# Query and key pieces stored once per batch, with the bias table loaded in eight portions between the stores

## The reference, cut to what matters

```
xn = layernorm(x)
Q, K, V = (proj(Wq, bq), proj(Wk, bk), proj(Wv, bv))      # (16, 16 heads, 256, 8)
scores = einsum('bhqd,bhkd->bhqk', Q, K) / sqrt(8) + rel_bias[:, clip(q - k, -128, 128) + 128]
out = softmax(scores) @ V
x = x + (out @ Wo.T + bo) * silu(ffn0(xn))
```

## Time and profile before

| | us |
|---|---|
| median of 3 timed runs | 816.46 (813.6 to 817.75) |
| the profiled execution, its own time | 811.98 |
| its span, first to last instruction | 809.9 |
| PE, DVE, ACT, POOL busy | 696.4, 555.7, 487.4, 454.5 |

### The profile page before, as it was taken

The page is one execution under the profiler, slowest core; times in us unless marked ns, Lnnn a source line. Parts: engine busy times, 40 slices in busy tenths (PEclk is TensorE's granted clock), DMA queues, the critical chain, the costliest instruction groups (busy, mean ns, idle before and its releaser), DMA issues. The chain is left out here.

```text
span 809.9 us, 16884 instructions
## 1 busy us (share of the span) xinstructions
PE 696.4 (86%) x5338; PEld 477.2 (59%) x5338; DVE 555.7 (69%) x1292; ACT 487.4 (60%) x919; POOL 454.5 (56%) x398
## 2 busy tenths in 40 slices
PE   2876888899998999979999889899897688999970
PEld 1652222233332333338999878789887677998870
DVE  7787999999997999843343377835737894643454
ACT  1662677788886888866455537578661264554550
POOL 8930454599998999983544544410005776554451
PEclk9898899999999999989999999999998799999995
DMA  7997551132332232136887796560001424777936
GB/s 234 362 275 220 171 172 54 54 95 79 90 97 72 80 91 76 57 125 193 247 261 246 240 308 195 175 176 1 2 1 37 156 75 113 238 220 232 290 122 194
DMA packets 115377, 124.09 MB, mean 153 GB/s; under 512 B 10608, under 2 KB 97312, under 8 KB 115328
## 3 DMA queue, kind: packets, MB, share of 16 engines
q1 hardware_dynamic: 107200, 106.71, 44.0%
q0 software_dynamic: 8128, 16.78, 5.9%
HBM read 82.50 MB, written 40.81 MB: 152 GB/s over the span
## 5 line engine op out<-in xcount | busy, mean ns | idle before, releaser
L696 POOL DMA_INDIRECT yg_dram<-work x138 | 137.3, 995 | 145.5 <-DVE work L1817 123.2
L1276 ACT ACTIVATE work<-wide,work 128x256 f32<-128x256 f32 x324 | 131.7, 474 | 112.4 <-PE wide L914 111.3
L1427 DVE TENSOR_REDUCE work<-wide 128x4 bf16<-128x1024 f32 x128 | 155.9, 1226 | 22.7 <-PE wide L791 21.7
L925 PE MATMUL wide<-work 128*128 128x128 f32 x1296 | 157.6, 275 | 0.0
L925 PEld LDWEIGHTS wide<-work 128*128 128x128 f32 x1296 | 151.6, 192 | 0.8 <-ACT work L1276 0.3
L914 PE MATMUL wide<-xT,work 128*128 128x256 f32 x552 | 132.0, 382 | 9.6 <-issue 7.1
L914 PEld LDWEIGHTS wide<-xT,work 128*128 128x128 f32 x552 | 99.5, 190 | 23.4 <-issue 10.7
L659 POOL TENSOR_TENSOR work<-work,biasT 128x1024 f32<-128x1024 f32 x32 | 75.9, 2371 | 53.5 <-ACT work L1214 53.1
L659 POOL TENSOR_TENSOR yy<-yy,biasT 128x1024 f32<-128x1024 f32 x32 | 75.8, 2368 | 21.6 <-ACT yy L1214 21.0
L1221 ACT ACTIVATE yy<-yy 128x1024 f32<-128x1024 f32 x64 | 67.5, 1055 | 29.9 <-DVE yy L1695 26.2
L785 PE MATMUL wide<-biasA,turnb 128*128 128x512 bf16 x256 | 80.4, 397 | 5.7 <-DVE work L1427 5.3
(11 more groups left out here) (288 smaller groups left out, 1202.0 us busy)
## 6 DMA issues: line engine op xcount, KB each, us to landing
work<-in_wcat SPq DMA_DIRECT2D x73, 578.0 KB, 4.0
work<-stk_dram SPq DMA_DIRECT2D x128, 96.0 KB, 2.7
xg_dram<-empty SPq DMA_DIRECT2D x35, 260.0 KB, 2.8
work<-xg_dram SPq DMA_DIRECT2D x69, 130.0 KB
stk_dram<-yy SPq DMA_DIRECT2D x16, 384.0 KB, 3.4
stk_dram<-yy SPq DMA_DIRECT2D x16, 256.0 KB, 3.2
yy<-yg_dram SPq DMA_DIRECT2D x8, 512.0 KB, 6.5
biasT<-ext_dram SPq DMA_DIRECT2D x1, 3072.0 KB
```

The source lines that it names most:

```text
L696: g.indirect_dma_start(out=yg_dram[l], out_offset=bass.IndirectOffsetOnAxis(ap=yid[v][:, s_:s_ + 1].bitcast(u32), axis=0), in_=yb[u][:, s_ ...
L925: last = mm(YP[u][:, s_ * D:(s_ + 1) * D], hb[u][:, c, s_ * P:(s_ + 1) * P], wb[v][:, HID + c * D:HID + (c + 1) * D], start=(c == 0), stop ...
L1276: A(hb[u][:, c, :], bank[2 + 2 * u + c // 2][:, (c % 2) * TS:(c % 2 + 1) * TS], ACT.Gelu, bias=wb[v][:, bc:bc + 1]).then_inc(m["gelu"], 1)
L1427: V.tensor_reduce(nmax[:, :, 2 * place(t):2 * place(t) + 2].rearrange("p c e -> p e c"), into[:, :].rearrange("p (e c k) -> p e c k", e=2, ...
```

## The change

1. The six pieces of a batch are stored once, by one transfer (six rows of 512 bytes for each of 128 partitions), instead of twelve pieces by three transfers.
2. The columns of the query and key projections are put into another order (feature first, then head), by one ACT copy of the weights into `wqk_dh` and a seventh small weight transfer that brings the two bias columns in that order. PE's first projection waits for the copy.
3. The stacks are put together by the loads, which read a piece as often as it is needed: for each parity of heads three transfers (24, 16 and 8 partitions), each for queries and keys at once, in runs of 2 KB. That is six transfers instead of four for each half of a batch's heads; the bytes are the same.
4. `biasT` is loaded in eight portions of two heads, one behind each of the stores of batches 0 to 7, instead of by one transfer ahead of all stores.
5. The loads for batches 0 and 1 go out in halves, one behind each store of batches 8 to 15, instead of whole ones behind the stores of batches 8 to 11.

```
-STORES = len(RUNS)
+LOADS = 2 * len(RUNS)
...
-    stk_dram = nc.dram_tensor("stk_dram", [2, NB * D, TERMS, S], bf16, kind="Internal").ap()
+    stk_dram = nc.dram_tensor("stk_dram", [NB, 2 * NPIECE, D, S], bf16, kind="Internal").ap()
...
+            sp.dma_start(more[:, 2:4], wpack[:, WPACK - 5:WPACK - 3].rearrange("(h d) i -> d h i", d=DK)).then_inc(s_w, 16)
...
-            sp.dma_start(biasT[:, :, :], bass.AP(tensor=ext_dram.tensor, offset=0, ap=[[1, P], [EXT, H0], [1, BW]])
-                         ).then_inc(s_bt, 16)
+
+            def load_biasT(q):
+                sp.dma_start(biasT[:, q * 2:q * 2 + 2, :],
+                             bass.AP(tensor=ext_dram.tensor, offset=q * 2 * EXT, ap=[[1, P], [EXT, 2], [1, BW]])).then_inc(s_bt, 16)
...
-                a, r = list(pieces[u].ap), 0
-                for n in RUNS:
-                    dst = stk_dram[:, b * D:(b + 1) * D, r:r + n, :].rearrange("i d r s -> d i (r s)")
-                    src = bass.AP(tensor=pieces[u].tensor, offset=pieces[u].offset, ap=[a[0], [(6 - n) * S, 2], [1, n * S]])
-                    sp.dma_start(dst, src).then_inc(pre[0][f"stored{u}"], 16)
-                    r += n
-
-            def load_stacks(b, u, g):
-                for e in range(2):
-                    rows = slice(e * HALF, e * HALF + TROWS)
-                    ts = slice(g * 4, g * 4 + 4)
-
-                    def src(i):
-                        heads = stk_dram[i, b * D:b * D + D] if isinstance(b, int) else stk_dram[i, bass.ds(b * D, D)]
-                        return heads.rearrange("(a e t d) r s -> a e (d r) t s", a=2, e=2, d=DK)[g, e]
-                    sp.dma_start(qst[u][rows, ts, :], src(0)).then_inc(A0[f"stk{u}{g}"], 16)
-                    sp.dma_start(kst[u][rows, ts, :], src(1)).then_inc(A0[f"stk{u}{g}"], 16)
+                sp.dma_start(stk_dram[b].rearrange("r p s -> p r s"), pieces[u]).then_inc(pre[0][f"stored{u}"], 16)
+
+            def load_stacks(b, u, g, halves=(0, 1)):
+                for e in halves:
+                    heads = stk_dram[b if isinstance(b, int) else bass.ds(b, 1)]
+                    row = e * HALF
+                    for n in RUNS:
+                        dst = qst[u][row:row + n * DK, g * 4:g * 4 + 4, :]
+                        sp.dma_start(
+                            bass.AP(tensor=dst.tensor, offset=dst.offset, ap=[list(dst.ap)[0], [H0 // 2 * S, 2], [1, 4 * S]]),
+                            bass.AP(tensor=heads.tensor, offset=heads.offset + (g * 2 + e) * 4 * S,
+                                    ap=[[H0 * S, n * DK], [(2 * NPIECE - n) * D * S, 2], [1, 4 * S]])
+                        ).then_inc(A0[f"stk{u}{g}"], 16)
+                        row += n * DK
...
             for b in range(NB // 2):
                 store_pieces(b, b % NRING)
+                load_biasT(b)
...
                 first = b - NB // 2
-                if first < 2:
-                    sp.wait_ge(pre[0][f"stored{first}"], len(range(first, NB // 2, NRING)) * STORES * 16)
-                if first < 4:
-                    load_stacks(first // 2, first // 2, first % 2)
+                if first % 4 == 0:
+                    sp.wait_ge(pre[0][f"stored{first // 4}"], len(range(first // 4, b, NRING)) * 16)
+                load_stacks(first // 4, first // 4, first // 2 % 2, (first % 2,))
...
+                        pe.wait_ge(s_wo, 1)
...
-                        last = mm(bank[6 + u][:, i * S:(i + 1) * S], wqk_sb[:, i * D:(i + 1) * D], xT[u][:, :],
+                        last = mm(bank[6 + u][:, i * S:(i + 1) * S], wqk_dh[:, i * D:(i + 1) * D], xT[u][:, :],
...
             act.wait_ge(s_w, 16 * NW)
+            A(wqk_dh[:, :].rearrange("p (i d h) -> p i d h", i=2, d=DK),
+              wqk_sb.rearrange("p (i h d) -> p i d h", i=2, d=DK), ACT.Copy).then_inc(s_wo, 1)
```

More of the change, by code:

```diff
@@ L67 @@
 RUNS = (3, 2, 1)
+NPIECE = max(RUNS)
 TERMS = sum(RUNS)
@@ L197, in build @@
         shb_bc = sb("shb_bc", [P, D])
-        more = sb("more", [P, 2])
+        more = sb("more", [P, 4])
+        wqk_dh = sb("wqk_dh", [P, 2 * D])
         ext_sb, extr_sb, extb_sb = (yyf[0:H0, TOK + 6 * S + i * EXT:TOK + 6 * S + (i + 1) * EXT] for i in range(3))
@@ L305, in build @@
         bank = [wide[i // 2][:, i % 2 * 512:(i % 2 + 1) * 512] for i in range(8)]
-        bq_c, bk_c, bv_c, nw_c, temp_c = (cols[:, i:i + 1] for i in range(5))
-        bqs_c, et_c = (more[:, i:i + 1] for i in range(2))
+        bv_c, nw_c, temp_c = (cols[:, i:i + 1] for i in range(2, 5))
+        bqs_c, et_c, bq_c, bk_c = (more[:, i:i + 1] for i in range(4))
         s_x = [sem(f"x{q}_loaded") for q in range(4)]
-        s_w, s_wf = sem("weights_loaded"), sem("weights_folded")
+        s_w, s_wf, s_wo = sem("weights_loaded"), sem("weights_folded"), sem("projections_ordered")
         s_c = sem("constants_made")
@@ L359, in build @@
         A1 = phase_sems("attend", 1, ["x2", "C", "Cs", "U", "pr", "nn", "nns", "G", "gk", "GT", "gm", "mx", "exp", "rs", "an", "M", "Ms", "Pm", "Ps", "F", "s"])
-        NW = 6
+        NW = 7
         NEMPTY = EMPTIES
@@ L434, in _ @@
                 first = b - NB // 2
-                if first < 2:
-                    sp.wait_ge(pre[0][f"stored{first}"], len(range(first, NB // 2, NRING)) * STORES * 16)
-                if first < 4:
-                    load_stacks(first // 2, first // 2, first % 2)
+                if first % 4 == 0:
+                    sp.wait_ge(pre[0][f"stored{first // 4}"], len(range(first // 4, b, NRING)) * 16)
+                load_stacks(first // 4, first // 4, first // 2 % 2, (first % 2,))
             for u in range(NRING):
-                sp.wait_ge(pre[0][f"stored{u}"], len(range(u, NB, NRING)) * STORES * 16)
+                sp.wait_ge(pre[0][f"stored{u}"], len(range(u, NB, NRING)) * 16)
             sp.wait_ge(s_fill, 3)
@@ L664, in attend_pool @@
                 pool.wait_ge(s_w, 16 * NW)
-                pool.wait_ge(s_bt, 16)
+                pool.wait_ge(s_bt, 128)
                 pool.wait_ge(pre[0]["sh"], NB + 2)
@@ L779, in max_scores @@
                 if t % 4 == 0:
-                    pe.wait_ge(a[f"stk{u}{t // 4}"], turn * 64 + 64)
+                    pe.wait_ge(a[f"stk{u}{t // 4}"], (turn + 1) * (LOADS * 16))
                 if early is None and (not isinstance(n, int) or n or t >= 2):
@@ L1771, in _ @@
                     route_shift(0)
-            dve.wait_ge(s_bt, 16)
+            dve.wait_ge(s_bt, 128)
             attend_dve(0, back=0, part=0)
@@ L1856, in beside_experts @@
                 elif j == NJA + 12:
-                    dve.wait_ge(s_bt, 80)
+                    dve.wait_ge(s_bt, 192)
                     add_gated(0)
```

2 lines of the change are left out of this document (1 added, 1 removed).

## The result

The changed kernel takes 806.62 us, median of 11 runs (804.91 to 812.08); the kernel before, in 11 runs beside them, 816.97 (813.6 to 817.75). The ratio is 0.989, with a 95% interval from 0.9873 to 0.9907: about 9 us less. The profiled execution took 807.83 us, its span is 805.7 and its mean granted clock 0.957 (before 809.9 and 0.955). In the profile two things have gone. One is 6.29 MB written to DRAM (40.81 to 34.52 MB), which is the second copy of the pieces. The other is 18,440 packets, and those are not the stores': a batch has 768 store packets in both kernels, of 512 bytes now. They are the loads': 24,584 packets under 2 KB have gone and 6,144 larger ones have come, since the stacks are now read in runs of 2 KB and not of 512 bytes (part 3).

The account below looks back on a forecast made before the run. Bound: in the projection stage DVE waits for ACT, and ACT for the stores of the pieces. Sum: 7.8 (gaps) + 1.0 (stage end) - 0.3 (backlog) = 8.5 us, so 816.46 - 8.5 = 808.0; range 804.5 to 813.5.

Parts of the forecast that it names:

- rival D: Whole kernel: the clock stays up and no gaps or backlog remain, gain 9.9 us, so 806.6; chance 0.07.
- The bound: Projection stage: DVE waits for ACT, which waits for the stores of the pieces; DVE loses 8.0 us.
- DVE's gaps, 7.8 us less: Projection stage: of DVE's 8.0 us of stalls all go but 0.2 us in the last four batches.
- The portions' backlog, 0.3 us: Projection stage, batches 0 to 7: queue falls behind 0.19 us a batch, 1.5 by batch 7; charged 0.3 us.
- The loads: Projection stage from batch 8: half a load adds 0.56 us a batch, or 0.75; the later waits go.
- The end of the stage, 1.0 us: Last piece to first exponent block, 8.17 us before: gain of 0.5 to 1.9 us, taken as 1.0.
- The weight copy and the seventh transfer, nothing: Kernel start: 0.4 us copy within ACT's 2.01 us wait, transfer with 1.8 us of cover; cost taken as 0.
- SP in the attention, nothing: Attention: six loads instead of four per half, 0.50 us each, covered by at least 1.5 us; no cost.
- Rival C: Attention: slower load issues make SP late, costing from 1.1 us an issue; 833 us at 1.7; chance 0.06.
- Rival A: Projection stores cost 33.5 ns a packet; ACT waits to 1 us in batches 6 to 9; 810 to 812; chance 0.18.
- rival B: Projection stage: 43.8 ns a packet whatever its size, 5.5 us of stall, gain 2.8, 813.7 us; chance 0.10.
- The end moves with 79.15: From the first exponent block at 79.15 us on: the kernel's end moves as that block does.

Follow-up runs that it names:

- e2: The changed kernel with the float32 bias table in one transfer ahead of all stores again; 810.76 us, ratio 0.9942 to the kernel before.
- e5: The changed kernel with each store issued twice, the other time into a DRAM tensor that nobody reads; 828.38 us, one run.
- f0: The changed kernel itself, run again on another chip; 807.35 us, ratio 0.9916 to the kernel before.
- e4: The changed kernel with every load of the stacks cut in two, twelve transfers instead of six per half; 856.17 us, one run on the slower chip.
- e1: The kernel before with only the bias table in eight portions behind the stores of batches 0 to 7; 820.35 us, ratio 1.0055.
- f6: The changed kernel with unread matrix products filling three idle stretches of TensorE; 805.54 us, ratio 0.9882 to the kernel before.
- e3: The changed kernel with the bias table in sixteen one-head portions, one behind each store of batches 0 to 15; 807.88 us, ratio 0.9905.
- f8: The changed kernel with two bias table portions ahead of the first store and unread products in three TensorE idle stretches; 805.74 us, ratio 0.9873.
- f7: The changed kernel with two of the eight bias table portions moved ahead of the first store; 809.45 us, ratio 0.992.
- e8: The same kernel as f8, on the slower chip; 850.44 us, ratio 0.9961 to the kernel before.
- e7: The same kernel as f7, on the slower chip; 844.02 us, ratio 0.9889 to the kernel before.

## Why the prediction held, point by point

Forecast 808.0 us, a gain of 8.5; measured 806.62, with a gain of 9.0 by the ratio and 10.35 by the two medians, of which 0.5 is that the kernel before has 816.97 in eleven runs and not 816.46. That the time falls on the 806.6 of rival D is luck: D wanted a clock that stays up and no gap at all, and the profile shows neither.

- **The bound.** The transfers paced DVE through ACT. Right: e2 (stores halved and loads changed, the table as before) takes all but 0.20 us of the five later gaps away, and e5 (stores doubled again, nothing else) brings ten back. How much of the later gaps the stores made and how much the old loads, no run shows.
- **DVE's gaps, 7.8 us less.** With the backlog's 0.3 that is 7.5 us; the gaps became 6.6 us less (8.0 to 1.4), the last piece came 6.95 us earlier. The later gaps were put at 0.2 and are absent in it, 0.20 in f0; the mechanism and the place (no wait at batch 3, none from batch 9 on) were right.
- **The portions' backlog, 0.3 us.** The step that was mis-sized: 1.36 us in this execution, 0.21 and 0.56 in f0. The reasoning had the right queue and a drift twice too large (0.19 a batch, measured 0.10), and still too small a stall. The first sign that it named failed: ACT was to wait no longer than 0.5 us for a store, and waited 1.88 at batch 8 and 0.55, 0.21 and 0.44 ahead of it, which is closer to the sign of A. What it lacked is that a single store can land late: the 16 stores landed 2.9 to 5.7 us after their issue, median 3.7, where the sum took 2.8 for an empty queue. The 2.8 is what e2's empty queue shows.
- **The loads.** Priced at 93 ns for 2 KB, or 0.56 us a batch, with 0.75 as the bound by a split over fewer engines. By the estimate above it is about 123 ns and 0.74 us, so the bound was the better figure, for whatever reason: no run shows the split. With the store that is 2.07 us a batch, less than DVE's 2.34, and there are no gaps behind ACT from batch 9 on.
- **The end of the stage, 1.0 us.** Measured 0.92 (8.17 to 7.25). PE's path was the last, as in the sum, at the lower clock; f0, with 6.30, shows the other end of the range that was given, 1.9. The last store landed 3.0 us after its issue (SP sends the first maxima at 67.08), against 3.2.
- **The weight copy and the seventh transfer, nothing.** Right in effect, off in size. The copy takes 0.67 us instead of 0.4, and ACT waits for the weights until 14.15 instead of 13.90; DVE's first difference is still at 21.88 in both.

ACT's timeline after (compare):

```profile
14.15 0.67 ACT L1124 ACTIVATE wqk_dh<-packed 128x256 f32<-128x256 f32 x1 [11.49 <-DMA more<-in_wpack]
...
41.45 0.63 ACT L1147 ACTIVATE yy<-work 128x512 bf16<-128x512 f32 x1 [1.88 <-DMA stk_dram<-yy]
```

- **SP in the attention, nothing.** Right, and with more room than thought: the loads are issued 0.42 us apart (2.38 us for six and their gaps), not 0.50. Rival C is refuted by the length of the attention, 274.84 us against 275.16, and e4 shows about where it would begin.
- **Rival A and rival B.** The price of the store packet decided between them: 27.8 ns in e2, 27.5 in the changed kernel. A needs 33.5 (its 1.8 us of stall should read 1.6, by 3.1 behind less 1.5 of room), B 43.8. What B describes is e1, where 43.8 ns is indeed the price, for packets of the old size.
- **"The end moves with 79.15."** Right up to the Gram products (leads of 7.87, 8.2 and 8.5 us at the attention's first and last block and at the first Gram product), and only partly behind them. The sum did not have what follows; the medians of 11 runs give the forecast gain all the same, because what follows is a difference between executions and not between the kernels, as far as the runs show.

## What was not expected: how long the low clock lasts

PE idles for 4.63 us at the start of the second layer's Gram products, and then runs at the lower clock. PE's timeline, before and after:

```profile
613.42 1.23 PE L1055 MATMUL wide<-biasT 128*128 128x128 f32 x4 [4.64 <-DVE biasT L1959]
...
642.25 0.47 PE L1080 MATMUL wide<-ident,biasT 128*128 128x128 f32 x1 [5.13 <-DVE biasT L2019]
```

```profile
604.89 1.22 PE L1059 MATMUL wide<-biasT 128*128 128x128 f32 x4 [4.63 <-DVE biasT L1965]
...
637.50 0.48 PE L1084 MATMUL wide<-ident,biasT 128*128 128x128 f32 x1 [5.23 <-DVE biasT L2025]
```

Of the lead of 8.53 us at the first row, 4.75 are left at the second. Nothing between them was touched by the change. The windows view of that stretch, before from 612 us on, and of 608 to 616 us of the changed kernel and of f6:

```profile
612.00:616.00 4.00, 2.58 (x10) 2.40 (x11) 2.56 (x11) 0.28 (x1) 2.98 (x3) 0.50 0.10 33
```

```profile
608.00:616.00 8.00, 8.00 (x34) 7.46 (x33) 3.71 (x17) 0.83 (x3) 6.17 (x7) 0.50 0.17 53
```

```profile
608.00:616.00 8.00, 8.00 (x63) 7.69 (x62) 6.73 (x31) 1.67 (x6) 6.02 (x7) 1.00 0.17 54
```

After the same idle time PE worked at the lower clock for 4.6 us in the execution of before (613.4 to 618.0) and for 12 us in the one of after (604.9 to 616.9); f6, with the idle time filled, had none, and did 63 products where the changed kernel did 34. From the first Gram product to the first transpose of similarities it takes 28.8 us before, 32.6 after, 31.3 in f0, 32.6 in e1, 30.2 in e2, 32.6 in e3, and 26.8 in both f6 and f8. So the two idle stretches of about 5 us cost 2 to 6 us together, and how much of it is not the kernel's doing: e2 and e3 run the same code there. The execution of before was a lucky one in this stretch, and its time is 811.98 us against a median of 816.97; the changed kernel's is 807.83 against 806.62.

The clock in this stretch is not all of it. From the attention's last exponent block to the first Gram product, with the same code in all kernels, it takes 259.1 us before, 258.8 after, 260.8 in f0, 261.5 in f7, 263.4 in f8 and 265.7 in e5. So a second stretch varies by as much; why is not shown. And f6, which has no lower clock in its Gram products, spreads over 8.4 us in six runs, no less than the changed kernel (7.2 us in eleven). A single profiled execution carries a few microseconds of this, in either direction, and a comparison of two spans (809.9 and 805.7, a gain of 4.2 where the medians give 9 to 10) would have told the wrong size.

The second surprise is the late store: 0 to 2 us at batch 8, in executions of kernels with the same transfers there (1.36 and 0.56; none in e8 and 2.02 in f8). The third is that one kernel takes 4.5% longer on another chip (853.5 against 815 to 817 us), at a lower mean granted clock (0.926 to 0.947 against 0.944 to 0.962 in the kernel before) and, in e7, with a batch of the attention at up to 17.7 us instead of 16.5.

## What to carry to other kernels

When a consumer waits for ring buffers to be stored, price the queue per packet by its size and set it against the producer's period: 768 packets took 2.10 us at a mean of 965 bytes and 1.33 at 512, in a period of 2.34 that the bias table's portions and the loads of the stacks share, and that difference, together with the loads' new size and place, brought 7.0 of the 7.9 us in the stage (e2). Part the two before you credit one. Splitting a large load between such stores helps only when the queue has air for it; with a full queue (e1) it turned six stalls into eleven and cost 2.4 us in the stage. Compare the same landmarks in both traces stage by stage, and look at the granted clock behind each idle stretch of TensorE of some microseconds before you credit or blame a change for the difference of two spans.
